# Cross-attention and routed experts on one core: paired logits of batch 0, maxima rows in one transfer, weights ahead, four gate places

## The reference

```python
q = split_heads(layernorm(x) @ Wq + bq); k = split_heads(ctx @ Wk + bk); v = split_heads(ctx @ Wv + bv)
logits = einsum('bhqd,bhkd->bhqk', q, k) / sqrt(16) + mask * -1e9
x = x + merge_heads(softmax(logits) @ v) @ Wo + bo
xf = layernorm(x).reshape(2048, 256)
weights, idx = top_k(softmax(xf @ w_gate), 2)          # 8 experts, capacity 1024 rows each
h = einsum('ecd,edf->ecf', rows_by_expert(xf, idx), c_fc)
a, g = split(h, 2); out = einsum('ecf,efd->ecd', silu(a) * g, c_proj)
x = x + sum over the two experts of weights * out
```

## Time and profile before

| | us |
|---|---|
| median of 3 runs | 420.84 (418.13 to 423.74) |
| the profiled execution | 421.77 |
| its span, first to last instruction | 419.7 |
| PE busy | 381.7 (91%) |
| DVE busy | 247.8 (59%) |
| ACT busy | 211.6 (50%) |
| POOL busy | 175.1 (42%) |
| mean granted clock of PE | 0.97 |

### The profile page before, as it was taken

The page is one execution under the profiler, slowest core; times in us unless marked ns, Lnnn a source line. Parts: engine busy times, 40 slices in busy tenths (PEclk is TensorE's granted clock), DMA queues, the critical chain, the costliest instruction groups (busy, mean ns, idle before and its releaser), DMA issues.

```text
span 419.7 us, 9490 instructions
## 1 busy us (share of the span) xinstructions
PE 381.7 (91%) x2864; PEld 304.8 (73%) x2865; DVE 247.8 (59%) x693; ACT 211.6 (50%) x336; POOL 175.1 (42%) x182
## 2 busy tenths in 40 slices
PE   7989999989989999999975899799899999999980
PEld 7765666656666656676743799699799999999970
DVE  6755358898988998889786365732232323232320
ACT  2355245566674756645467368334354545454530
POOL 5833233626737384450623026722333334334331
PEclk9999699999999999999999699989999999999996
DMA  7357454793958869392245224644333323333330
GB/s 218 82 117 165 116 115 145 239 219 125 217 150 204 242 156 200 111 224 79 77 153 204 75 52 101 130 87 88 64 55 56 63 44 54 62 53 65 59 50 4
DMA packets 61593, 49.54 MB, mean 118 GB/s; under 512 B 11695, under 2 KB 58471, under 8 KB 61543
## 3 DMA queue, kind: packets, MB, share of 16 engines
q1 hardware_dynamic: 53577, 40.29, 37.8%
q0 software_dynamic: 7008, 8.43, 12.4%
q10 hardware_dynamic: 976, 0.41, 0.4%
HBM read 31.30 MB, written 18.28 MB: 118 GB/s over the span
## 4 chain that ended last, share of the span: by engine, by line
PE 66%; DMA 13%; issue 7%; DVE 4%; ACT 4%; SPq 2%; POOL 2%; ACTq 0%; POOLq 0%; DVEq 0%
PE bank L1191 21%; PE bank L1202 10%; PE bank L1106 6%; PE bank L976 6%; DMA out<-CTt,GG 4%; PE bank L1063 4%; PE bank L993 3%; PE bank L1024 3%; DMA wf<-NMT 3%; PE bank L1076 3%; PE bank L1089 3%; DVE NEG L1344 2%; PE bank L1171 2%; PE bank L984 2%; PE bank L955 2%
## 5 line engine op out<-in xcount | busy, mean ns | idle before, releaser
L1191 PEld LDWEIGHTS bank<-CX,KS 128*128 128x128 f32 x912 | 110.6, 197 | 6.9 <-issue 5.2
L1191 PE MATMUL bank<-CX,KS 128*128 128x128 f32 x912 | 111.5, 280 | 3.3 <-issue 3.2
L842 ACT ACTIVATE PR<-bank 128x512 f32<-128x512 f32 x128 | 73.4, 591 | 54.8 <-PE bank L1089 38.8
L730 POOL DMA_INDIRECT out<-CTt,GG x38 | 58.9, 1549 | 96.9 <-DMA out<-CTt,GG 67.5
L1344 DVE TENSOR_REDUCE NEG<-bank 128x2 f32<-128x512 f32 x112 | 75.4, 684 | 26.4 <-PE bank L1063 25.2
L902 ACT ACTIVATE KS<-wf 128x1536 f32 x40 | 59.2, 1483 | 43.5 <-PE bank L1191 43.0
L1619 DVE COPY CX<-bank 128x256 f32<-128x256 f32 x39 | 16.5, 424 | 82.6 <-PE bank L1171 82.5
L1202 PE MATMUL bank<-wp,QF 128*128 x228 | 56.0, 382 | 1.8 <-DVE CTt L1633 1.8
L640 POOL DMA_INDIRECT slots<-R,slot x32 | 32.8, 1026 | 37.2 <-DVE slot L1476 18.1
L1202 PEld LDWEIGHTS bank<-wp,QF 128*128 128x128 f32 x228 | 40.3, 190 | 6.4 <-issue 2.5
L908 ACT ACTIVATE KF<-bank 128x384 f32<-128x384 f32 x38 | 18.6, 491 | 44.6 <-PE bank L1191 44.6
(11 more groups left out here) (188 smaller groups left out, 526.2 us busy)
## 6 DMA issues: line engine op xcount, KB each, us to landing
wf<-in_L_ffn_c_fc SPq DMA_DIRECT2D x8, 768.0 KB, 5.5
XG<-slots SPq DMA_DIRECT2D x40, 128.0 KB, 2.4
wp<-in_L_ffn_c_proj SPq DMA_DIRECT2D x8, 384.0 KB, 5.4
kparts_d<-KP SPq DMA_DIRECT2D x7, 384.0 KB, 2.5
KS<-kparts_d SPq DMA_DIRECT2D x7, 384.0 KB
KS<-kparts_d SPq DMA_DIRECT2D x21, 128.0 KB
qparts_d<-QP SPq DMA_DIRECT2D x7, 384.0 KB, 3.3
wf<-qparts_d SPq DMA_DIRECT2D x6, 384.0 KB
```

The lines of the kernel that those rows point to most:

```text
L730: pool.indirect_dma_start(out_rows, bass.IndirectOffsetOnAxis(ap=GG[:, u, 1:2].bitcast(U32), axis=0), Y[:, u, :], None, bounds_check=last_ ...
L842: act.activation(PR[:, s % NPROB, :], STB[s % 2][:], ACT.Exp).then_inc(exp_done, 1)
L1191: ins = pe.matmul(bank[2 + 2 * u + g][:, c * P:(c + 1) * P], UP[u][:, (k * 2 + g) * FF + c * P:(k * 2 + g) * FF + (c + 1) * P], XTG[:, u, ...
```

## The change

1. **Batch 0's logits.** `direct_logits` takes two units at once, four matmuls in the order unit, next unit, unit, next unit, so that neighbours lie on different 32-row groups and in different banks. It waits until both exponentials of the pair before are done. V of batch 0 is made ahead of NM0 and ahead of the units, and ACT evacuates it and takes the second part of batch 1's queries ahead of the first exponential. The projections of batch 2 come one unit earlier (`AT_SECOND`), and within a unit ACT evacuates ahead of taking second parts of keys.
2. **Maxima rows.** NM0 moves from unit 11 to unit 10 and to the front of its unit; `max_rows` is one transfer of three rows for three of one row.
3. **Last weights.** `load_weights(B - 1)` goes ahead of `max_rows(B - 1, 1)` on SP.
4. **Blocks.** GG has four places for blocks 0 to 10; the down product alternates between bank 1 and bank 6 from block 5 on; `blocks_table` is cut in two on DVE and spread over two blocks; the pad rows go out three, three and two, behind blocks 8, 9 and 10 and their gates, and gates 9 and 10 go ahead of the wait for the pad rows.

```diff
@@
-    "NM0": 11, "NM1": 2, "PF": 3, "V": 4, "WO": 6, "X2": 12, "LG": 13, "BO": 12,
+    "NM0": 10, "NM1": 2, "PF": 3, "V": 4, "WO": 6, "X2": 12, "LG": 13, "BO": 12,
@@
-AT_SECOND = {"CT": 1, "K": 2, "XT": 3, "Q": 4, "second K": 5, "second Q": 8}
+AT_SECOND = {"CT": 0, "K": 1, "XT": 2, "Q": 3, "second K": 4, "second Q": 7}
@@
-    return pieces + [(kind, it + rel) for kind, rel in MISC_PLAN if unit == place(kind, it) and 0 <= it + rel]
+    planned = [(kind, it + rel) for kind, rel in MISC_PLAN if unit == place(kind, it) and 0 <= it + rel]
+    return [p for p in planned if p[0] == "NM0"] + pieces + [p for p in planned if p[0] != "NM0"]
@@
+def gate_place(t, u):
+    return t % GATES if not later(t, PEELED - 1) else u
+def two_banks(t):
+    return later(t, 5)
...
+        def down_bank(t, u):
+            return MISC[0] if u == 1 and two_banks(t) else bank[1]
@@
-                for j in range(3):
-                    sp.dma_start(query_rows(n)[R_MAX + j:R_MAX + j + 1, 8 * half:8 * half + 8, :],
-                                 NMT[8 * j:8 * j + 8, half, :]).then_inc(nm_in[half], 16)
+                sp.dma_start(query_rows(n)[R_MAX:R_END, 8 * half:8 * half + 8, :],
+                             NMT[0:24, half, :]).then_inc(nm_in[half], 16)
@@
-                if later(t, 2):
+                if later(t, PEELED - 1):
                     sp.wait_ge(added[u], (t - u) * 8)
-                sp.dma_start(GG[:, u, :], slots[bass.ds(row, P), D:RW]).then_inc(gg_in[u], 16)
+                elif later(t, GATES):
+                    sp.wait_ge(added[u], (t - GATES - u) * 8 + 16)
+                sp.dma_start(GG[:, gate_place(t, u), :], slots[bass.ds(row, P), D:RW]).then_inc(gg_in[u], 16)
@@
+            padded = {8: range(0, 3), 9: range(3, 6), 10: range(6, E)}
+            for t in range(4, AHEAD):
                 load_block(t, t % 2)
-                load_gates(t - 3, (t - 3) % 2)
-                if t == AHEAD - 4:
+                if t > GATES:
+                    load_gates(t - 1, (t - 1) % 2)
+                if t == 8:
                     sp.wait_ge(pad_at_ready, 1)
-                for e in range(2 * (t - AHEAD + 4), 2 * (t - AHEAD + 5)) if t >= AHEAD - 4 else ():
+                for e in padded.get(t, ()):
                     pad_expert(e)
@@
+            evacuate("V", 0)
+            second_of_queries(1)
             for it in ITERATIONS[:-1]:
@@
-                if u >= 2:
-                    pe.wait_ge(exp_done, u - 1)
+                if first >= 2:
+                    pe.wait_ge(exp_done, first)
                 for i in range(2):
-                    ins = pe.matmul(STB[u % 2][:, i * S:(i + 1) * S], KZ[rows, i, hp // GROUPS, c * P:(c + 1) * P],
-                                    QZ[rows, i, hp // GROUPS, :], start=True, stop=True)
-                ins.then_inc(st_ready, 1)
+                    for u in (first, first + 1):
+                        hp, c = u // QUAD * 2 + u % 2, u // 2 % 2
+                        rows = slice(2 * DH * (hp % GROUPS), 2 * DH * (hp % GROUPS + 1))
+                        ins = pe.matmul(STB[u % 2][:, i * S:(i + 1) * S], KZ[rows, i, hp // GROUPS, c * P:(c + 1) * P],
+                                        QZ[rows, i, hp // GROUPS, :], start=True, stop=True)
+                        if i == 1:
+                            ins.then_inc(st_ready, 1)
@@
-                if later(t, 1):
+                if two_banks(t):
+                    pe.wait_ge(ys_ready, t - 1)
+                elif later(t, 1):
                     pe.wait_ge(ys_ready, t)
@@
             step(5, 1)
+            rest_experts()
+            step(6, 0)
             rest_table()
-            step(6, 0)
+            step(7, 1)
             rest_pairs()
```

More of the change, by code:

```diff
@@ L82 @@
     "residual": 7, "stats2": 8, "stats1": 11, "normalize2": 10, "choice": 14, "counted": 15,
-    "gates": 1, "bias": 11, "first V": 0, "stats1 of 3": 8,
+    "gates": 1, "bias": 11, "stats1 of 3": 8,
 }
 LAST_MISC = {0: [("PF", B - 3)], 1: [("NM1", B - 1)], 3: [("CNT", KNOWN)], 6: [("WO", B - 2)]}
+GATES = 4
 TAIL_MISC = [("X2", B - 2), ("WO", B - 1), ("LG", B - 2), ("PF", B - 2), ("X2", B - 1),
@@ L150, in misc_at @@
     pieces = [(kind, n) for kind in PROJECTION for n in projected_at(it, unit, kind)]
-    if it == 0 and unit == AT["first V"]:
-        pieces.insert(0, ("V", 0))
     if it == 0 and unit == AT["BO"]:
@@ L563, in _ @@
             load_block(1, 1)
-            load_gates(0, 0)
-            load_gates(1, 1)
+            for t in range(GATES):
+                load_gates(t, t % 2)
             store_rows(B - 2)
@@ L795, in evacuate @@
                     if n >= 2:
-                        act.wait_ge(nm_in[half], 48 * (n - 1))
+                        act.wait_ge(nm_in[half], 16 * (n - 1))
                     act.activation(NMT[:, half, :], src[0:24, 0:S // 2].bitcast(BF16), ACT.Copy).then_inc(nmt_ready[half], 1)
@@ L871, in _ @@
                     exponentials(it, u)
-                    if it == 0 and u == 1:
-                        second_of_queries(1)
-                    for n in second_at(it, u, "second K"):
-                        second_of_keys(n)
                     for kind, n in misc_at(it, u):
@@ L880, in _ @@
                             first_part(kind, n)
+                    for n in second_at(it, u, "second K"):
+                        second_of_keys(n)
                     if u == AT["copy rows"] and 0 <= it - 1:
@@ L1145, in _ @@
             misc("Q", 1)
+            misc("V", 0)
             misc("NM0", 0)
@@ L1151, in _ @@
                         row_max_logits(it + 1, w)
-                    if it == 0:
+                    if it > 0:
+                        logits(it, u)
+                    elif u % 2 == 0:
                         direct_logits(u)
-                    else:
-                        logits(it, u)
                     if it == 0 and u == 2:
@@ L1482, in running, with blocks_experts @@
                 link(dve.tensor_reduce(dst, cum8[:], AX.X, ALU.add))
-            def blocks_table(incl, weight, first, n, extra, done):
+            def blocks_experts(incl, weight, n):
                 b = blk_no[:, 0:n]
@@ L1492, in blocks_table @@
                 link(dve.tensor_reduce(bex[:, 0:n], leb[:, 0:n], AX.X, ALU.add))
+            def blocks_table(first, n, extra, done):
+                b = blk_no[:, 0:n]
                 link(dve.scalar_tensor_tensor(out=btmp[:, 0:n], in0=bexp[:, 0:n], scalar=float(REGION // P), in1=b,
@@ L1670, in _ @@
             step(5, 1)
+            rest_experts()
+            step(6, 0)
             rest_table()
-            step(6, 0)
+            step(7, 1)
             rest_pairs()
-            for t in range(7, PEELED):
+            for t in range(8, PEELED):
                 step(t, t % 2)
```

36 lines of the change are left out of this document (15 added, 21 removed).

## The result

The changed kernel takes 414.75 us (median of 20 runs, 410.64 to 419.31); the kernel before, beside it, 420.86 us (415.99 to 425.66). The ratio is 0.9871, 95% interval 0.9842 to 0.9901: 1.3% faster, where 403 us (4.3%) was forecast with a range from 396 to 413; the measured time lies outside it. The profiled execution has a span of 411.8 us for 419.7.

What follows compares the result with a forecast made beforehand. The prediction took TensorE's work, plus its waits and low-clock stretches, as the bound. Terms summed to -18.2 from 421.77 us, giving 403.6, or 402.7 against the median; forecast 403, range 396 to 413.

Steps and rivals of the forecast that it cites:

- the third term: Maxima rows: transposes moved to unit 10 and one transfer for three, -1.0 us (+4 to -5).
- the wait of about 0.7 goes: Batches 1 to 6, ahead of a logits unit: maxima rows land some 3 us earlier, ending TensorE's wait for them.
- Weights ahead: -4.0: Start of blocks: last two weight loads leave the scatter's way, blocks start 2.8 us earlier, clock gives 2.5; -2.8 to -5.3.
- the landing in 3.2: Ahead of the blocks: the last scatter lands in 3.2 us, at 226.1 for 228.88.
- Batch 0: -5.0 and -2.2: Logits of batch 0: units 0 to 7 gain 5.0 us (3.6 to 6.4), units 8 to 15 gain 2.2 (0 to 4.3).
- landing of rows at 39.5: Batch 0, unit 6: query rows of batch 1 landed at 39.5 us for 42.06, 2.6 gained.
- half a clock: Batch 0, around unit 6: half the time lost to the lower clock counted as regained, 1.35 us.
- DVE then binds: Batch 0, units 8 to 15: DVE's work sets the time at about 15.2 us, from 17.6.
- Peeled blocks: -6.0: Peeled blocks: two holes close, by the table in two pieces and by earlier gates; range -3 to -7 us.
- Steady blocks: zero: Steady blocks and tail: no gain, as the last gates still wait for an add.
- given back: Rival: batch 0's gain is lost again, units 8 to 15 yield nothing, batch 1 stands 2 us; 415 us, chance 0.12.
- Slower: Rival: TensorE's clock stays down through batch 0; 434 us, chance 0.04.

Runs made afterwards that it cites:

- after: The changed kernel itself, all parts of the change against the kernel before: 414.75 us, ratio 0.9871.
- after_again: The changed kernel run once more, unedited, beside other kernels: 414.91 us, ratio 0.9925 to the kernel before.
- back_three: Changed kernel with the transposes of the first half's maxima back at unit 11 and the maxima rows in three DMAs again: 407.57 us.
- before_nm0: Kernel before with only the transposes of the first half's maxima moved to the front of unit 10: 427.13 us for 421.78, ratio 1.0189.
- group 2: Runs made beside each other: kernel before 423.73 us, changed kernel unedited 414.91 us, and three edited versions of the changed kernel.
- split_early: Changed kernel with DVE's split of the first half's maxima at unit 8 instead of 9: 409.19 us.
- split_mended: Changed kernel with the split at unit 8, query parts written before the key rows' read, and pad rows ahead of gates: 412.53 us for 428.13, ratio 0.9651.
- v_early: Changed kernel with V of batch 1 at unit 5 of batch 0 instead of unit 7: 414.95 us.
- pads_first: Changed kernel with SP writing the pad rows ahead of the wait for the gates from block 9 on: 411.72 us.

## Why the prediction was wrong

The gains by stage, read from the starts of WO and of the hidden layers in the profiles (us, negative is faster):

| | forecast | after | after_again |
|---|---|---|---|
| to WO of batch 0 | -7.2 | -3.8 | -5.0 |
| to WO of batch 5 (maxima rows) | -1.0 | +2.8 | +4.4 |
| to hidden layer 1 (weights ahead) | -4.0 | -4.8 | -2.7 |
| to hidden layer 13 (peeled blocks) | -6.0 | -2.0 | -3.7 |
| to the end | 0 | 0.0 | +0.2 |

**What failed** is the third term, "maxima rows: -1.0 (+4, six iterations that buy nothing, to -5)". The working had both halves: TensorE waits 0.9 for the split less 0.25, and a wait of 0.7 goes. The first half was nearly right from batch 2 on: a stand of 0.91 in batches 2 to 4, and a period 0.88 longer than with unit 11. Two steps were not.
- I took "the wait of about 0.7 goes" as a gain. It went, 2.8 us in four waits, and DVE's NEG took its place with 2.7 in four. DVE was busy 88.2 of 100 us from 75 to 175 in the kernel before; TensorE at 92.7 hid that it was near. back_three shows the exchange: with NMT or with NEG the batches take the same.
- I scaled the stand from one batch. In batch 1 it is 2.0 and not 0.9, since the last operation of the split takes 1.27 us beside POOL, and in six of the eight profiles with the transposes there and in front K then ran at the lower clock (3.5 to 3.7 us for 1.99; not in those of after and before_nm0). The row was in the trace of before too (L1384 at 84.11, 1.27 long), in a batch I didn't look at.

The term is +5.1 (414.9 less 409.8), up to +8 by before_nm0's ratio, where the sum had -1.0: of the 11.8 us missed it makes 6.1 by the medians.

**Weights ahead: -4.0 was between 0 and -1.6 for the order alone.** The stage gave more, -4.8 and -2.7, and the 2.1 between these two is the clock behind the routing (0.95 for 0.87 over the stretch), in which after was lucky. The step that failed is to charge the order alone with the gain: with the single transfer SP comes to the loads sooner anyway, and each of the two edits does by itself what both do. And the landing in 3.2 was too good: 3.6 to 4.6 us pass from the last scatter to the read where no weights are in the way.

**Batch 0: -5.0 and -2.2.** Alone it measured -7.2 by the medians (-2.0% by the ratio) and -2.6 by the profile; in after and after_again batch 1's first unit starts 3.1 and 4.3 earlier. In units 0 to 7 the failed step is the landing of rows at 39.5: I gave the write its usual 2.45 although the sentence before had SP issue the key rows until 28.27. It took 4.95. TensorE thus stood 3.74, no cover for half a clock. In units 8 to 15 the -2.2 was -0.4 in after and -1.4 in after_again. The step "DVE then binds" holds only in part: DVE was busy 12.2 of the 17.3 us and not full, TensorE waited 1.1 for NEG and 0.68 for an exponential, and behind two of these waits the clock fell in after, which the sum had at nothing; that is most of the 1.1 between the two profiles. The pairs are worth 3.0 in all.

**Peeled blocks: -6.0** was -2.0 in the profile of after, -3.7 in after_again and -3.4 alone (-5.3 by the medians, -1.9 by the ratio). The two holes closed as worked out; the one at the pads, named as a sign of failure, opened, and with the pads put first layer 1 to 13 takes 54.6 for 60.2, -5.6. I had weighed which gates come before the pads, and not that SP, standing for gates 8, would then write pads ahead of the next block's rows. (The first hole was also counted from two kinds of rows: 4.54 in the timeline less 2.68 in the chain; by the timeline's own 2.84 it is 4.06 and not 4.2. In the same way four times 1.05 are 4.2, where the term for units 8 to 15 says 4.3.)

**Steady blocks: zero**, right.

Taken apart, medians give -7.2, -5.3, +5.3 and -1.4, together -8.6; the whole measured -6.1 with 20 runs and -8.8 in group 2. The ratios of the first three are -2.0%, -0.4% and +1.9%, for -1.3% and -0.8% of the whole. The parts add within what the groups tell. Of the rivals, "given back" at 415 had the number, in part by luck: units 8 to 15 gave little and batch 1 stood 2 us, as it said, but that stand was for the split and not for rows, and DVE ate the maxima rows' gain in batches 1 to 5. "Slower" didn't come: the clock stayed up but for short dips.

## What to carry to other kernels

A wait that you remove pays only up to the next engine's bound: read that engine's busy time over the same stretch, and expect its waits to come up in place of the old ones. An instruction put in front of others on an in-order engine is charged with its worst wait in any iteration, not with the one looked at; check every iteration for it. Where two edits may cure the same wait, undo them singly and together: singly, each looks worthless. Compare stages of two profiles only beside their granted clocks. On a queue, put what needs no waiting (here pad rows) before what waits, and what is needed first ahead of what is merely ready first.

## What the hardware did that was not expected

- DVE's last split operation, 16 elements in 0.17 us, took 1.27 when POOL's tensor_tensor on 512 (1.26 us) started 0.02 us earlier; both ended together. It did so in batch 1 of 18 of the 20 profiles and took 0.17 to 0.20 in the other batches; in split_early and split_mended, where it comes 2.3 us ahead of POOL's, it took 0.17 to 0.18 in batch 1 too.
- The granted clock fell behind short waits: in 11 of the 16 profiles with paired logits behind the 0.57 and 0.68 us in units 11 and 12 of batch 0 (BO then took up to 2.08 us for 1.13), and not in the other five, which stood as long; the four without pairs have neither the waits nor the dip. It fell after a stand of 2.2 us in v_early, and after the 2.0 in batch 1 in some executions and not in others (K took 1.99 in the profile of after, 3.50 in that of pads_first). Such dips go with the spread of one kernel's runs: mean granted clock 0.978 at 410.6 us and 0.961 at 416.6 among after's twenty.
- Behind four reads of 768 KB together in the same queue a write of 384 KB took 4.95 us instead of 2.45; moved ahead of them, it gave that time to the read that follows, which took 7.69 for 6.24.
